# Attention with cached keys and a routed low-rank layer on one core: scores over 544 keys in one pass, two pairs ahead, with another order of gathers, masks, weight halves and first loads

## What is computed

```python
q = rope(rmsnorm(x @ Wq.T)); k = rope(rmsnorm(x @ Wk.T)); v = x @ Wv.T      # 32 query heads, 8 key heads, head size 128
k_all = concat([k_cache[block_table], k], axis=1)                           # 512 cached keys, then 32 own ones
v_all = concat([v_cache[block_table], v], axis=1)
scores = q @ k_all.T * SCALE, masked to cached index < cache_seqlen         # own keys always count
o = softmax(scores) @ v_all;  x = x + o @ Wo.T
base = x @ W.T;  gates = top-2 softmax of (x @ Wr.T + language bias)
x = x + base + 2 * sum_e gates_e * (x @ A_e.T) @ B_e.T
```

## Time and profile before

| what | value |
|---|---|
| runs, median of 3 (lowest, highest) | 1454.44 us (1452.36, 1454.81) |
| profiled execution, its span from first to last instruction | 1451.3 us |
| busy PE, DVE, POOL, ACT | 93%, 78%, 67%, 53% |
| mean granted clock of PE | 0.982 of full speed |
| median from issue to landing of a gather | 3.7 us |

### The profile page before, as it was taken

One profiled execution on the slowest core, in us unless ns is written; L12 is line 12 of the kernel. 1 busy time (PEld: TensorE's weight loads), 2 busy tenths in 40 slices (PEclk: granted clock), 3 DMA queues, 4 the chain that ended last, 5 costly groups with the idle time before them and its releaser, 6 DMA issues.

```text
span 1451.3 us, 28498 instructions
## 1 busy us (share of the span) xinstructions
PE 1356.5 (93%) x8640; PEld 1162.0 (80%) x8640; DVE 1132.6 (78%) x2891; ACT 766.9 (53%) x1989; POOL 973.1 (67%) x1269
## 2 busy tenths in 40 slices
PE   2599999998999999999999999999999999999889
PEld 1478888887878888887777888888787888888777
DVE  6688877777887778788877878887888888777754
ACT  1356555555664555556554555666555556555431
POOL 5676777777766677776766777777777777676500
PEclk8699999999999999999999999999999999999999
DMA  6434444454543343436533433445544343435401
GB/s 228 133 87 121 133 119 134 123 173 133 173 117 116 125 119 125 135 108 202 164 117 107 138 112 112 128 125 181 170 142 129 104 129 117 131 122 167 124 22 58
DMA packets 61380, 188.72 MB, mean 130 GB/s; under 512 B 10736, under 2 KB 11504, under 8 KB 58608
## 3 DMA queue, kind: packets, MB, share of 16 engines
q0 software_dynamic: 40960, 134.25, 31.3%
q1 hardware_dynamic: 19504, 53.50, 10.5%
q10 hardware_dynamic: 864, 0.46, 0.1%
HBM read 177.95 MB, written 12.32 MB: 131 GB/s over the span
## 4 chain that ended last, share of the span: by engine, by line
PE 69%; DVE 21%; issue 5%; ACT 2%; DMA 1%; DVEq 1%; POOL 0%; SPq 0%; ACTq 0%; POOLq 0%
PE PROJ L182 13%; PE MISC L182 13%; PE O L359 10%; PE S L182 10%; PE PT L349 8%; PE KT L338 5%; DVE probs L736 4%; PE O L361 3%; DVE scores L729 2%; PE PROJ L328 2%; DVE kT_lo L750 2%; DVE rope_v L703 2%; PE PROJ L330 2%; DVE mask L716 2%; DVE rope_u L699 2%
## 5 line engine op out<-in xcount | busy, mean ns | idle before, releaser
L976 POOL DMA_INDIRECT kv_rows<-in_kv,step_idx x512 | 529.8, 1035 | 219.6 <-issue 117.8
L550 ACT ACTIVATE pT<-PT 128x640 f32<-128x640 f32 x256 | 180.2, 704 | 300.6 <-PE PT L349 300.6
L359 PEld LDWEIGHTS O<-pT,kv_rows 128*128 128x128 f32 x2048 | 262.6, 192 | 27.0 <-ACT pT L550 9.8
L359 PE MATMUL O<-pT,kv_rows 128*128 128x128 f32 x2048 | 274.8, 277 | 2.9 <-ACT pT L550 2.6
L546 ACT ACTIVATE kT_hi<-KT 128x512 fp32r<-128x512 f32 x256 | 151.2, 590 | 225.1 <-PE KT L338 225.0
L750 DVE TENSOR_TENSOR kT_lo<-KT,kT_hi 128x512 fp32r<-128x512 f32 x256 | 176.0, 687 | 71.3 <-ACT kT_hi L546 70.7
L554 ACT ACTIVATE probs<-scores,min_all 128x640 f32<-128x640 f32 x256 | 212.7, 831 | 23.3 <-DVE min_all L729 21.0
L349 PEld LDWEIGHTS PT<-ident,probs 128*128 128x128 f32 x1280 | 142.1, 141 | 89.9 <-DVE probs L736 78.7
L349 PE MATMUL PT<-ident,probs 128*128 128x128 f32 x1280 | 191.3, 280 | 22.7 <-DVE probs L736 22.3
L729 DVE CUSTOM_DVE_ANT_0 scores<-S,mask,min_new 128x512 f32<-128x512 f32 x256 | 190.5, 744 | 0.0
L182 PE MATMUL PROJ<-w_hi,x_hi 128*128 128x512 f32 x384 | 172.0, 448 | 15.0 <-DVE w_lo L663 12.6
(11 more groups left out here) (215 smaller groups left out, 2702.6 us busy)
## 6 DMA issues: line engine op xcount, KB each, us to landing
stage<-in_wqkv SPq DMA_DIRECT2D x12, 1024.0 KB, 7.7
x_raw<-in_xT SPq DMA_DIRECT2D x32, 256.0 KB, 4.2
stage<-in_wo SPq DMA_DIRECT2D x8, 1024.0 KB, 6.6
kv_rows<-in_kv,step_idx POOLq DMA_INDIRECT x512, 3.7
y_tile<-y_running SPq DMA_DIRECT2D x32, 256.0 KB, 3.7
y_running<-y_tile SPq DMA_DIRECT2D x31, 256.0 KB, 2.1
out<-kv_rows SPq DMA_DIRECT2D x8, 256.0 KB, 2.0
stage<-in_w1T SPq DMA_DIRECT2D x1, 1024.0 KB, 6.7
```

Source lines behind the costliest of these rows:

```text
L359: nc.tensor.matmul(O[:, 0:P], kv_rows[:, b, c, GK * D + h * D:GK * D + (h + 1) * D], pT[:, c * P:(c + 1) * P], start=c == 0, stop=False)
L550: nc.scalar.activation(pT[:, :], PT[:, 0:KEYS], ACT.Copy).then_inc(sm["pT_ready"], 1)
L976: G.indirect_dma_start(kv_rows[:, b, c, :], None, kv[:, :], bass.IndirectOffsetOnAxis(ap=step_idx[:, b * LC + c:b * LC + c + 1], axis=0)). ...
```

## The change

- **Scores.** The own keys stand behind the 512 cached ones in a kT of 544 keys, with four slots (`SLOTS`), so one `score` makes all 544 in six passes (three of 288 columns, three of 256). `new_scores`, the two reductions and the small copy per pair go. `fill_slots` copies the own keys into four slots at a time, twice a tile. Exponentials and division run over 544 columns in place of 640.
- **Distances.** On every engine, scores are made two pairs ahead, and keys turned three pairs ahead (`turn_keys(i, p + 3)`). So the next tile's row 0 is turned at p = 5, row 1 at p = 7. The projection chunks are spread otherwise (`fill`): block 0 at p = 0, block 1 at p = 1 and 2, block 2 at p = 3 and 4. PE's part of a tile begins with `turn_probs(i, 0)`.
- **Masks.** All 32 masks are made once, kept in device memory as bf16 and loaded per half tile by SP (`load_mask`).
- **POOL.** `keep_v` writes the own values masked per row (128x1024 in place of 128x256). All four gathers of a row are issued together; row 0's come after two rotated blocks, row 1's after the third block and the table of the tile after next.
- **Weights.** Loads, roundings and rests go in halves of 512 KB, on ACT and DVE alone, spread over the last two tiles of a group and the first of the next; the second layer's weights too.
- **Start.** The block table is loaded first, the indices are made before the angles, and the first weight blocks are rounded by ACT.

Cut to its core:

```diff
-                score(i, 0)
-                turn_kv(i, 1)
-                project_some(0)
-                for p in range(PAIRS - 1):
-                    score(i, p + 1)
-                    turn_probs(i, p)
-                    if p + 2 < PAIRS:
-                        turn_kv(i, p + 2)
...
+                for p in range(PAIRS):
+                    turn_probs(i, p)
+                    if p + 3 < PAIRS:
+                        turn_keys(i, p + 3)
+                    elif not last:
+                        turn_keys(i + 1, p + 3 - PAIRS)
+                    if p + 2 < PAIRS:
+                        score(i, p + 2)
+                    elif not last:
+                        score(i + 1, p + 2 - PAIRS)
+                    for k, c in fill[p] if not last else []:
+                        proj(i + 1, k, (c, 1), wcount)
...
+                for j0, j1 in score_parts:
+                    k_hi, k_lo = (kT[:, p % SLOTS, z, j0:j1] for z in range(2))
+                    mm = three_pass(SX[:, SX_AT + j0:SX_AT + j1], lambda c: (q_hi, q_lo), lambda c: (k_hi, k_lo), 1, 0, 0)
...
+                keep_v(i)
+                b = ROWS - 1
+                take_indices(t, b, b + 1, 2 * i + 2)
+                gather(b, 0, LC)
...
+                def next_values(b):
+                    pool.wait_ge(sm["pv_done"], CREDIT + i * PAIRS + b * GK + GK)
+                    pool.nop(nofuse=True)
+                    gather(b, 0, LC)
+
+                for k in range(2):
+                    make_rstd(i + 1, k)
+                    rotate_sum(i + 1, k)
+                for row in range(ROWS - 1):
+                    pool.wait_ge(kv_in[row], (i + 1) * 16 * LC)
+                take_indices(tn, 0, ROWS - 1, 2 * i + 3)
+                next_values(0)
+                make_rstd(i + 1, 2)
+                rotate_sum(i + 1, 2)
+                if not (final and fixed and t == TILES - 2):
+                    make_table(i + 2, (t + 2) % TILES if fixed else t + 2)
+                next_values(1)
+                next_values(2)
```

More of the change, by code:

```diff
@@ new lines, in body @@
+                if not last:
+                    load_mask(i + 1, tn, 0)
+                if not final and fixed and t == TILES - 2:
+                    next_half(g + 1, 2)
+                    next_half(g + 1, 3)
+                if before_last:
+                    load_l1(2)
+                    load_l1(3)
+                if not final and fixed and t == TILES - 1:
+                    next_half(g + 1, WO_FIRST)
+                    next_half(g + 1, WO_FIRST + 1)
+                if not last:
+                    load_mask(i + 1, tn, 1)
@@ new lines, in body @@
+                if not final and fixed and t == TILES - 2:
+                    next_half(g + 1, 4)
+                if fixed and t == 0:
+                    if final:
+                        load_l1(0)
+                        load_l1(1)
+                    else:
+                        next_half(g + 1, 0)
+                        next_half(g + 1, 1)
+                if last:
+                    for b in range(ROWS):
+                        n = 1 if b == ROWS - 1 else 2
+                        sp.wait_ge(sm["pv_done"], CREDIT + i * PAIRS + b // 2 * GK + GK)
+                        sp.dma_start(y_all[:, 2 * b:2 * b + n, :], y_rows[2 * b:2 * b + n, :, :].rearrange("t p n -> p t n")
+                                     ).then_inc(l1_y_in[b], 16)
@@ new lines, in body @@
+                for p in range(PAIRS):
+                    if p + 1 < PAIRS:
+                        normalise(i, p + 1)
+                    elif not last:
+                        normalise(i + 1, 0)
+                    if p + 2 < PAIRS:
+                        minimum(i, p + 2)
+                    elif not last:
+                        minimum(i + 1, p + 2 - PAIRS)
+                    if p == 1:
+                        fill_slots(i, 1)
+                    if p + 3 < PAIRS:
+                        rest_kT(i, p + 3)
+                    elif not last:
+                        rest_kT(i + 1, p + 3 - PAIRS)
+                    if not last:
+                        if p in (1, 2, 4):
+                            rotate(i + 1, p // 2)
+                        if p == 5:
+                            rest_qT(i + 1, 0)
+                            rest_kT_new(i + 1)
+                            fill_slots(i + 1, 0)
+                        if p == 6:
+                            rest_qT(i + 1, 1)
@@ L880, in body @@
                     take_o(i, p)
                     if fixed:
[L882 to L884 removed]
+                        rest_weights(g, t, p, final)
                 if not (final and fixed and t >= TILES - 2):
                     split_x(i + 2)
[L887 to L890 removed]
@@ L1109, in body @@
-                if not last:
-                    keep_v(i + 1)
+                keep_v(i)
+                b = ROWS - 1
+                take_indices(t, b, b + 1, 2 * i + 2)
+                gather(b, 0, LC)
+                if last:
+                    return
+                if fixed and t == TILES - 1:
+                    G.tensor_scalar(row_base[:, :], row_base[:, :], float(TOKENS_CACHED), 0.0, ALU.add, ALU.add
+                                    ).then_inc(sm["base_ready"], 1)
+                    pool.wait_ge(sm["base_ready"], g + 1)
```

852 lines of the change are left out of this document (417 added, 435 removed).

## The result

The changed kernel takes 1668.1 us (median, 1662.4 to 1681.3) where the kernel before took 1454.6 beside it: ratio **1.149 [1.144, 1.153]**, slower by 15%. The profiled execution took 1681.3 us, its span 1679.5. Measured again for experiment 5, the same kernel came to 1667.5, ratio 1.146 [1.144, 1.149]. One execution in all was disturbed, the profiled one of experiment 11 (2686 us beside 1469 to 1478 for its other four), and its ratio leaves it out.

The account below looks back on a forecast made before the run. The prediction took late gathers, through POOL's chain to row 1's landing, to bound the changed kernel: 57 + 31 x 48.0 + 75 = 1620 us span, median 1623 us, slower by 12%, range 1510 to 1700.

Parts of the forecast that it names:

- Steps 1 to 3: From PE's turn_probs(i, 0) at T: projection, squares at T+15.1, POOL's work and transfers, row 0 landed at T+27.8.
- Step 4: PE, at the turning of row 0's keys at p = 5, arrives at T+23.2 and waits 4.6 us.
- Step 5: POOL goes on with third block, table and row 1's transfers; row 1 lands at T+38.9.
- Step 6: PE reaches row 1's keys at p = 7 at T+34 to 35 and waits 4 to 5 us again.
- the section on the clock: Two PE clock falls a tile after its waits; the first comes out of the second wait, the second costs 1.3 us.
- Step 7 and the clock: PE's work from row 1's landing to the next T at T+46.7; with the clock fall 48.0 us per tile.
- The claim that the chain runs through POOL: POOL's serial work and transfers from the squares to row 1's landing, 23.8 us, make PE wait; chance 0.80.
- Gains on PE: Small passes gone, scores and projections cheaper: about 37.7 us per tile for a PE never waiting for a gather.
- The serial piece: DVE's five instructions at p = 5 before the next tile's score 0, some 3 us; put at 1 us per tile.
- the other rival: Gathers just in time, PE stays the bound: 38.7 us per tile, 1335 us, faster by 8%; chance 0.12.
- Start and end: Time to tile 0's first turned probabilities, 57 us, and from tile 31's to the end, 75 us.
- the last part on group ends: Half blocks' work at group ends falls into slack on ACT or DVE: nothing, at most 15 us over the run.

Follow-up runs that it names:

- experiment 5: The changed kernel itself, without an edit, measured again on another chip than the first four follow-ups: 1667.5 us, ratio 1.146 to the kernel before.
- experiment 11: Changed kernel with row 0's transfers behind the key block, row 1's around the second query block, table last, repeated on another chip: ratio 1.015.
- 10: Changed kernel with 18 and 16 throwaway transposes on PE ahead of its two waits for gathered keys, repeated on another chip: 1633.0 us, ratio 1.123.
- 6: Changed kernel with POOL's table of row positions made behind row 2's transfers, repeated on another chip: 1578.5 us, ratio 1.086.
- 2: Changed kernel with row 0's transfers behind the key block, row 1's around the second query block, table last: 1501.3 us, ratio 1.016.
- 7: The order of 2 on POOL, with the sum of the two rotated halves moved from POOL to DVE: 1416.9 us, ratio 0.975.
- experiment 12: Kernel of 7 with three of row 1's transfers ahead of the second query block and one behind, not two and two: 1411.1 us, ratio 0.971.
- 9: Changed kernel with splits of the next group's query, key and value weights cut to 16 of 512 columns: 1656.7 us, ratio 1.141.
- 13: Kernel of 9 with half-block weight loads behind the first group also cut to 32 of 512 columns: 1648.7 us, ratio 1.133.
- experiment 1: Changed kernel with POOL's table of row positions made behind row 2's transfers, first run, on the chip with late starts: 1740.6 us, ratio 1.176.
- the kept-busy one: Changed kernel with throwaway transposes on PE ahead of its two waits for gathered keys: 1688.6 us, ratio 1.143; repeated on another chip as 10, 1.123.
- rows early: The POOL order of 2, run on two chips: ratio 1.016 in 2 and 1.015 in experiment 11.

## Why the prediction was right, and where its sizes were off

The direction and the mechanism held: 15% slower against the 12% predicted (1623 us). By its steps:

- **Steps 1 to 3** (squares T+15.1, row 0 landed T+27.8): T+15.5 and T+28.0. The transfer took the 3.7 us of the old trace. The 2.6 us by the Trainium skill's page "DMA: Bandwidth & Descriptors", section "Anatomy of one DMA — SWDGE (gpsimd) path", would have put it at T+26.9; the trace decides.
- **Step 4** (PE waits 4.6 from T+23.2): 4.33 from T+23.7.
- **Step 5** (row 1 landed T+38.9): T+39.15.
- **Step 6** (PE waits 4 to 5 again): 2.3 to 3.6. The first fall of the clock put PE at T+36 to 37, not 34 to 35, which the section on the clock had foreseen ("taken out of the second wait"). It cost nothing, since the end of that wait is set by POOL.
- **Step 7 and the clock** (46.7, and 1.3 for a second fall, 48.0): 47.0 without and 48.5 with the fall; the 19 steady tiles of experiment 5 have a mean of 47.95, close to the 48.0 predicted, and that close by luck: the tile without the fall was put 0.3 too low, and the fall, 1.5 us in 11 of 19 tiles or 0.9 in the mean, 0.4 too high. That the second fall alone counts is shown by 10 beside the short tiles of 5.
- **The claim that the chain runs through POOL** is shown by 6, 2, 7: a shorter chain or an earlier place in it gives back 6, 13 and 17% without a change in PE's work.
- **Gains on PE** (38.7 for a PE that never waits for a gather: 37.7 of work and 1 for the serial piece): experiment 12 has 40.1, of which 1.4 us are waits, so 38.7 of work. The serial piece is this 1.4, with the sums of the rotation on DVE as well. So the other rival's 38.7 was 1.4 too low; in this kernel it lay hidden behind the gathers. The columns of the score came out as read: 288 take 0.13 us from start to start (739.67 to 739.80 in the trace after), and a score of six passes 0.83 behind transposes.
- **Start and end** (57 and 75): 59.5 and 75.6.

**The step that was mis-sized** is the last part on group ends: "nothing, at most 15 us". In the profiled execution the nine tiles 6 to 8, 14 to 16 and 22 to 24 took 40.7 us more than 48 each, in experiment 5 37. The term stood in the trace before and was read there: "the ends of the three groups cost some 43 more". The same nine tiles take 39.8 us more than 40.4 each in it. The sum then dropped it, since I put the half blocks' splits into slack beside a waiting PE. POOL's chain has no slack between the squares and row 1, and it was held up at several places: at the squares (by DVE splits in tiles 7, 15 and 23, and by a first pair of PE that took 1 to 4 us longer in tiles 8 and 16), at the index copy by a DVE split (9), and at the landings beside 512 KB loads (13). Nor is POOL all of it: in experiment 12, where PE hardly waits for a gather, these nine tiles still stand 27 us above 40.1 each, with small waits for ACT and DVE. A good part of the 37 has no cause shown.

Of the rest, the 21 tiles that are neither 0 nor at a group's end add 10 us in the profiled execution, most of it in the steady tiles 5, 12, 25 and 27 with 50.0 to 50.5 us, where the granted clock was 0.50 over the four us from T+39.2, in place of 0.57 to 0.67 or 1.00 in the other steady ones. Tile 0 with 53.4 us adds 5, start and end 3. That makes the 59.5 us between a span of 1620 and one of 1679.5; against the median of the changed kernel 45 are missing.

The rival on the other side (gathers just in time, 1335 us) needed row 1 at T+34.5. It did not come to be in this order of POOL, and experiment 12, another order with the sums on DVE, shows what it might have been worth: 1411, not 1335. Of the 76 us between, 31 x 1.4 = 43 are the serial piece and 27 the group ends.

## What to carry to other kernels

When a loop's consumer is moved earlier (keys turned three ahead in place of fewer), walk the producer's queue from the last thing it waits for to the landing and compare it with the new time of use, before counting what the consumer gains: here under 2 us a tile were saved on PE, and some 9 lost to waits and clock. Work that stands ahead of a transfer on its queue and isn't needed for it (a table, a sum that another engine can make, a block's product) is the cheap thing to move. Where an engine waits twice in a period, ask which fall of the clock anything waits for; here it was only the one behind the last wait. Ends of groups that cost time in the trace before should stay in the sum until something is shown to remove them, and work added to "idle" engines must be checked against the one engine in the chain that has no slack.

## What the runs showed of the hardware that was not expected

- On one chip, and in none of the traces from elsewhere, the work that follows PE's passes began late with no releaser in the profile, in a steady place of the tile: 3.67 us from the pass to DVE's start in experiment 1, 0.52 in the same kernel on another chip. That it is the raise of PE's semaphore that comes late is the reading of these rows; what makes it late on that chip was not tried. It made that kernel 1.176 in place of 1.086, the kept-busy one 1.143 in place of 1.123, and rows early no slower (1.016, 1.015). A ratio to a reference on the same chip did not take it out, because it hit kernels by different amounts; the changed kernel itself had to stand beside its experiments.
- In the steady tiles of experiment 5 a second wait of 2.4 to 3.5 us brought a fall of the clock in 11 of 19 and not in 8, with the same work ahead of it, often in turns; the first wait, of 4.0 to 4.5 us, brought it every time. In experiment 6 the granted clock was 1.00 over the five us behind all 19 second waits of 0.3 to 1.4 us, and 0.66 to 0.72 behind the four of 2.0 to 3.3.
- Two tiles of 32, 6 and 19, have the pause of POOL inside row 0's transfers (3.0 us from one to the next in place of 1.4) in every trace that was read, that of the kernel before too, and the profile names no releaser.
